# Second attention with keys on partitions: shifts in the f16 product, fp32 values and ones in column tiles, no transposes, and a reordered feed-forward

## The reference, cut to what matters

```python
q = (x @ Wq.T)                       # 8 heads of 32
kv = x @ Wkv_down.T                  # rank 64
k, v = kv @ Wk_up.T, kv @ Wv_up.T
scores = einsum('bqhd,bkhd->bhqk', q, k) * 32 ** -0.5
attn = softmax(scores, axis=-1)      # over 1024 keys
out = einsum('bhqk,bkhd->bqhd', attn, v) @ Wo.T
```

## Time and profile before

| | |
|---|---|
| median of 3 runs | 2518.78 us (2516.68 to 2521.06) |
| the profiled execution: time, span | 2519.22 us, 2517.4 us |
| granted TensorE clock, mean | 0.938 of 2.4 GHz |
| busy share of the span: PE, DVE, ACT, POOL | 87%, 84%, 72%, 49% |
| second attention, first load to the projection's first load | 1753.85 to 2320.67 us |
| first and second feed-forward, and the store of the result | 1526.2 to 1678.6 us, 2356.6 us to the end |

### The profile page before, as it was taken

The page is one execution under the profiler, slowest core; times in us unless marked ns, Lnnn a source line. Parts: engine busy times, 40 slices in busy tenths (PEclk is TensorE's granted clock), DMA queues, the critical chain, the costliest instruction groups (busy, mean ns, idle before and its releaser), DMA issues. The chain is left out here.

```text
span 2517.4 us, 62298 instructions
## 1 busy us (share of the span) xinstructions
PE 2198.9 (87%) x22572; PEld 1502.4 (60%) x22572; DVE 2116.7 (84%) x3170; ACT 1817.7 (72%) x2658; POOL 1239.9 (49%) x1482
## 2 busy tenths in 40 slices
PE   5899999999999999999999983556899999999464
PEld 3466667666667666667666663442455555555444
DVE  6899999999999999999999967755899999996674
ACT  1788888888888888888888860115899999996011
POOL 3444444444444444444444443200888888885120
PEclk9999999999999999999999996659899999999766
DMA  2799999999999999999999990006232222221001
GB/s 91 123 192 193 192 186 193 192 192 190 190 192 193 188 192 193 187 193 191 193 190 188 193 172 24 0 8 218 61 72 70 69 71 70 69 69 40 24 1 34
DMA packets 1183690, 333.53 MB, mean 132 GB/s; under 512 B 1145968, under 2 KB 1174512, under 8 KB 1183216
## 3 DMA queue, kind: packets, MB, share of 16 engines
q1 hardware_dynamic: 1182320, 326.97, 73.0%
q10 hardware_dynamic: 1152, 3.62, 0.4%
HBM read 30.57 MB, written 14.68 MB: 18 GB/s over the span
## 5 line engine op out<-in xcount | busy, mean ns | idle before, releaser
L329 PE MATMUL a_out_ps<-a_vs,a_pT 128*128 128x129 f16 x4096 | 726.0, 221 | 48.2 <-ACT a_own_out L378 46.7
L416 DVE SCALAR_TENSOR_TENSOR a_parts<-a_probs,a_parts 128x1024 f16<-128x1024 f32 x512 | 653.2, 1276 | 115.5 <-ACT a_parts L369 115.5
L333 PE MATMUL a_out_ps<-a_vs,a_pT 128*128 128x129 f16 x4096 | 724.4, 219 | 0.0
L331 PE MATMUL a_out_ps<-a_vs,a_pT 128*128 128x128 f16 x4096 | 724.3, 218 | 0.0
L361 ACT ACTIVATE a_probs<-a_score_ps,a_negmax 128x1024 f32<-128x1024 f32 x512 | 572.1, 1117 | 164.9 <-DVE a_negmax L410 164.9
L410 DVE TENSOR_REDUCE a_negmax<-a_score_ps 128x1 f32<-128x1024 f32 x512 | 621.3, 1213 | 2.5 <-PE a_score_ps L315 2.4
L369 ACT ACTIVATE a_parts<-a_probs 128x1024 f16<-128x1024 f32 x512 | 543.4, 1061 | 0.6 <-DMA a_pT<-a_parts 0.6
L329 PEld LDWEIGHTS a_out_ps<-a_vs,a_pT 128*128 128x128 f16 x4096 | 396.5, 97 | 146.1 <-ACT a_own_out L378 99.7
L331 PEld LDWEIGHTS a_out_ps<-a_vs,a_pT 128*128 128x128 f16 x4096 | 403.0, 98 | 44.6
L477 POOL TENSOR_TENSOR acc<-acc,a_own_out 128x256 f32<-128x256 f32 x256 | 248.3, 970 | 351.9 <-DVE a_parts L416 346.5
L311 PE MATMUL a_score_ps<-kh,a_qs 128*128 128x512 f16 x1024 | 388.6, 379 | 10.3 <-DVE a_qs L401 7.0
(11 more groups left out here) (200 smaller groups left out, 2737.0 us busy)
## 6 DMA issues: line engine op xcount, KB each, us to landing
a_pT<-a_parts SPq DMA_TRANSPOSE x512, 4.9
b_qs<-q_parts SPq DMA_DIRECT2D x128, 64.0 KB, 2.0
b_ks<-k_parts SPq DMA_DIRECT2D x128, 64.0 KB, 1.8
q_parts<-b_parts SPq DMA_DIRECT2D x32, 128.0 KB, 1.9
k_parts<-b_parts SPq DMA_DIRECT2D x32, 128.0 KB, 1.9
v_parts<-b_v_all SPq DMA_DIRECT2D x4, 1024.0 KB, 4.6
b_vs<-v_parts SPq DMA_DIRECT2D x32, 128.0 KB, 2.0
b_sent_pT<-b_sent_parts SPq DMA_TRANSPOSE x256, 2.3
```

The lines of the kernel that those rows point to most:

```text
L329: pe.matmul(out[:, 0:D + 1], hi, vs[:, G % 2, 0, j, 0:D + 1], start=j == 0, stop=False, skip_group_check=True)
L331: pe.matmul(out[:, 0:D], hi, vs[:, G % 2, 1, j, 0:D], start=False, stop=False, skip_group_check=True)
L333: last = pe.matmul(out[:, 0:D + 1], lo, vs[:, G % 2, 0, j, 0:D + 1], start=False, stop=j == JB - 1, skip_group_check=True)
L416: dve.scalar_tensor_tensor(out=parts[:, T % RING_P, 1, :], in0=probs[:, T % RING_P, :], scalar=PSCALE, in1=parts[:, T % RING_P, 0, :], op0 ...
```

## The change

`attend_b` is new. A unit is still 512 queries of one head, 64 in all, but its loops are written out. For each unit:

- `rate(u, t)`: for 128 queries, the scores against 1024 keys, queries on partitions, in the one tile max_ps; 96 rows of the stack (three pairs of parts). `row_max` takes the negated maximum of it (4 for each unit), and that is all that these scores are used for. After the fourth, the maxima are scaled into nm16 (f16, divided by 64).
- `spread_max`: four short products put the maxima of 512 queries on all partitions of bank 3 of score_ps; `keep_shift` copies 32 rows of it into rows 96 to 127 of qs. The same rows of ks hold 2, so that the score product subtracts the shift.
- `scores(u, pair)`: keys on partitions, 512 queries, two blocks of 128 keys for each of four pairs; `exponentiate` has no bias and no row sum, and writes fp32 probabilities that are already turned.
- `times_v(u, pair)`: for both blocks, v (fp32, kept on chip by `prepare_b` in v_all) and a block of ones are the stationary operands of four column tiles of 32 each. The ones give the denominator. `keep` takes the reciprocal of 128x128 denominators and multiplies.

GpSimd only writes two constants. Maxima run up to two units ahead. oT has the queries' four tiles on four groups of 32 partitions; `project_b` multiplies them as 32 products a chunk in four row tiles, with Wo loaded by eight DMAs.

`prepare_b` keeps v as fp32: no low parts, no store.

In the feed-forward, xh waits for the scoring products; the third `turn` moves behind the last pick, and the copy of xsel ahead of the last four of ohT; ScalarE scales half of kx, from a second product with the key weights; the normalising moves behind the product with v; the gate is one Silu activation and one product.

```diff
-def attend_b(st, q_dram, k_dram, v_dram, oT, ident):
+def attend_b(st, q_dram, k_dram, v_all, oT, ident):
...
+        max_ps = st.ps(s, "b_max_ps", [P, SEQ])
+        score_ps = st.ps(s, "b_score_ps", [P, 4, HALF])
+        out_ps = [st.ps(s, f"b_out_ps{i}", [P, 2, 2 * P]) for i in range(2)]
...
+            def rate(u, t):
...
+                if t == 0 and u % 2 == 0:
+                    pe.wait_ge(qk_in[slot], 96 * (u // 2 // SLOTS + 1))
+                if u or t:
+                    pe.wait_ge(max_ready, TILES * u + t)
+                cols = slice(u % 2 * HALF + t * P, u % 2 * HALF + (t + 1) * P)
                 for c in range(2):
+                    last = pe.matmul(max_ps[:, c * CH:(c + 1) * CH], qs[0:STACK, slot, cols],
+                                     ks[0:STACK, slot, c * CH:(c + 1) * CH], start=True, stop=True)
+                last.then_inc(rated, 1)
+
+            def spread_max(u):
...
+                pe.wait_ge(nm_ready, u + 1)
+                if u:
+                    pe.wait_ge(exp_done, PARTS * (u - 1) + 2)
+                for t in range(TILES):
+                    last = pe.matmul(score_ps[:, 3, t * P:(t + 1) * P], nm16[:, u % 2, t:t + 1].broadcast_to([P, P]),
+                                     ident16[:], start=t == 0, stop=True, skip_group_check=True)
+                last.then_inc(spread, 1)
+
+            def scores(u, pair):
+
+                if pair == 0:
+                    pe.wait_ge(shift_ready, u + 1)
+                if pair == 3 and u + 1 < units:
+                    pe.wait_ge(shift_ready, u + 2)
+                if u or pair >= 2:
+                    pe.wait_ge(exp_done, PARTS * u + pair - 1)
+                slot = u // 2 % SLOTS
+                for j in (2 * pair, 2 * pair + 1):
+                    last = pe.matmul(score_ps[:, j % 4, :], ks[:, slot, j * P:(j + 1) * P],
+                                     qs[:, slot, u % 2 * HALF:(u % 2 + 1) * HALF], start=True, stop=True)
                 last.then_inc(scored, 1)
...
+            def times_v(u, pair):
...
+                if pair == 0 and u >= 2:
+                    pe.wait_ge(kept, u - 1)
+                pe.wait_ge(exp_done, PARTS * u + pair + 1)
+                out = out_ps[u % 2]
+                for j in (2 * pair, 2 * pair + 1):
+                    for kind, left in ((0, v_all[:, u // 2, j, :]), (1, ones[:])):
+                        for t in range(TILES):
+                            last = pe.matmul(out[t * HDB:(t + 1) * HDB, 0, kind * P:(kind + 1) * P], left,
+                                             probs[:, u % 2, j, t * P:(t + 1) * P], start=j == 0 and kind == 0,
+                                             stop=j == JB - 1, skip_group_check=True)
                 last.then_inc(pv_done, 1)
...
+            for u in range(units):
+                scores(u, 0)
+                scores(u, 1)
+                rate(u + 1, 3)
+                times_v(u - 1, 2)
+                times_v(u - 1, 3)
+                spread_max(u + 1)
+                rate(u + 2, 0)
+                scores(u, 2)
+                scores(u, 3)
+                rate(u + 2, 1)
+                times_v(u, 0)
+                times_v(u, 1)
+                rate(u + 2, 2)
...
+            keep_shift(0)
+            for u in range(units):
+                exponentiate(u, 0)
+                exponentiate(u, 1)
+                keep_shift(u + 1)
+                exponentiate(u, 2)
+                exponentiate(u, 3)
...
+            for u in range(units):
+                row_max(u + 1, 3)
+                row_max(u + 2, 0)
+                keep(u - 1)
+                row_max(u + 2, 1)
+                row_max(u + 2, 2)
+            keep(units - 1)
...
             pool.wait_ge(ln.normed, NT)
+            pool.wait_ge(junked, NT)
             pool.tensor_tensor(xh[:], x[:], xn[:], ALU.add)
...
-                dve.tensor_tensor(pr_[:, pr], pr_[:, pr], rd[:, pr, :, None].broadcast_to([P, HA, CAP]),
-                                  ALU.mult).then_inc(probs_ready, 1)
             dve.wait_ge(o_done, 1)
-            dve.tensor_copy(o[:], A[:, 0:2 * D].rearrange("p (r d) -> p r d", r=2)).then_inc(o_kept, 1)
+            dve.tensor_tensor(o[:].rearrange("p r (h d) -> p r h d", h=HA),
+                              A[:, 0:2 * D].rearrange("p (r h d) -> p r h d", r=2, h=HA),
+                              rd[:, :, :, None].broadcast_to([P, 2, HA, HDA]), ALU.mult).then_inc(o_kept, 1)
...
-            act.activation(e[:], wide[0][:, 0:6 * QK].rearrange("p (c t) -> p c t", c=3), ACT.Exp,
-                           scale=-1.0).then_inc(up_exped, 1)
+            act.activation(e[:], wide[0][:, 0:6 * QK].rearrange("p (c t) -> p c t", c=3),
+                           ACT.Silu).then_inc(up_gated, 1)
...
+                for h in range(HB):
+                    u = 2 * (c // 2 * HB + h) + c % 2
+                    for t in range(TILES):
+                        rows = slice(t * HDB, (t + 1) * HDB)
+                        last = pe.matmul(y[c % 2][:, t, 0:D], oT[rows, u, :], wo[rows, h, :], start=h == 0,
+                                         stop=h == HB - 1)
```

More of the change, by code:

```diff
@@ L495, in _ @@
                     add((i - AH - 4) // 2)
-def attend_b(st, q_dram, k_dram, v_dram, oT, ident):
+def attend_b(st, q_dram, k_dram, v_all, oT, ident):
     nc = st.nc
     heads = NB * HB
[L509 to L523, removed]
-    with ExitStack() as s:
[L526 to L559, removed]
-        v_ready = st.sem("b_v_ready")
-        pool_passed, sp_passed = st.sem("b_pool_passed"), st.sem("b_sp_passed")
@@ L619, in _ @@
+            for G in range(heads):
+                slot = G % SLOTS
+                if G >= SLOTS:
+                    sp.wait_ge(scored, 2 * PARTS * (G - SLOTS + 1))
+                for part in range(3):
+                    rows = slice(part * HDB, (part + 1) * HDB)
+                    sp.dma_start(qs[rows, slot, :], q_dram[part // 2, G]).then_inc(qk_in[slot], 16)
+                    sp.dma_start(ks[rows, slot, :], k_dram[part % 2, G]).then_inc(qk_in[slot], 16)
         @block.tensor
         def _(pe):
[L621 to L635 removed]
@@ L693, in one_turn @@
-            def one_turn(n, first, last):
-                for t in range(TURN_T):
-                    if not (last and t + AHEAD_B >= TURN_T):
-                        scores(n, t + AHEAD_B)
-                    for j in (2 * t, 2 * t + 1):
-                        if j % JB not in SENT:
-                            turn(n, j)
-                        if not (first and j < LAG):
-                            times_v(n, j - LAG)
-            for t in range(AHEAD_B):
-                scores(0, t)
@@ new lines, in _ @@
+            pe.wait_ge(consts, 3)
+            for t in range(TILES):
+                rate(0, t)
+            spread_max(0)
+            for t in range(TILES - 1):
+                rate(1, t)
+            for u in range(units):
[12 more added lines that the diff above has]
+                rate(u + 2, 2)
@@ L792, in one_turn @@
-            def one_turn(n, first, last):
-                for t in range(TURN_T):
-                    if not (last and t + AHEAD_B >= TURN_T):
-                        row_max(n, t + AHEAD_B)
-                    for j in (2 * t, 2 * t + 1):
-                        if j in splits:
-                            low(n, j)
-                        elif j in dve_js:
-                            copy_block(n, j)
-                    if not (last and t + AHEAD_B > TURN_T):
-                        invert(n, t + AHEAD_B - 1)
-                    if t % 4 in (1, 2) and not (first and t < 4):
-                        keep(n if t >= 4 else n - 1, (t // 4 - 1) % UNITS, t % 4 - 1)
@@ new lines, in keep @@
+            def keep(u):
+                if u < 0:
+                    return
+                dve.wait_ge(pv_done, PARTS * (u + 1))
+                dve.reciprocal(inv[:, u % 2, :], out_ps[u % 2][:, 0, P:]).then_inc(inv_ready, 1)
+                dve.wait_ge(inv_ready, u + 1)
+                dve.tensor_tensor(oT[:, u, :], out_ps[u % 2][:, 0, 0:P], inv[:, u % 2, :], ALU.mult).then_inc(kept, 1)
+            dve.memset(ks[STACK:P, :, :], SHIFT / HDB).then_inc(consts, 1)
+            for t in range(TILES):
+                row_max(0, t)
```

398 lines of the change are left out of this document (105 added, 293 removed).

## The result

The changed kernel takes 2492.52 us (median of 3 runs, 2492.05 to 2493.61) against 2518.78: a ratio of 0.9894, 95% interval 0.9879 to 0.991. It is 26.3 us faster; 2492 was forecast. The profiled execution has a span of 2490.3 us against 2517.4.

A forecast was written before the change was run, and what follows sets the result against it. TensorE was taken to bound the second attention, other engines near behind, and chains of single steps the feed-forwards and projection. From 2519.22 us, +22.5 - 3 - 8 - 39 = -27.5 gave 2492, range 2458 to 2530.

The forecast's parts named there:

- The loop: Second attention: products and row maxima wait for each other through the single max_ps, so a unit takes 8.9 us.
- The first rival: Second attention: blocks of eight column-tile groups bind harder, 0.03 more a group erases the gain; typical 2535 us, chance 0.2.
- the second: Rival: blocks of column-tile groups don't bind, unit 8.55 us, projection 1.7 a chunk; total 2466 us, chance 0.18.
- Second attention: Whole attend_b stage: start, 62 full units of 8.9 us and end sum to 589 against 566.8, +22.5 us.
- Preparation: prepare_b: without the store of v the next stage waits only for the last k store, -3 us.
- Projection: project_b: 32 products in row tiles, 2.2 us a warm chunk, and eight loads for one; 26.6 against 34.6, -8 us.
- Feed-forward: Both feed-forwards: shorter chains of single steps save 19.5 us each, -39 us together.
- xh: Feed-forward: GpSimd's sum moved behind the scoring products lets the transposes end 8.7 us earlier and stays hidden.
- The normalising: Feed-forward: the second group of transposes need wait only for the second exponential, -4.3 us.
- the gate: Feed-forward, before the w3 products: a silu and one product replace a reciprocal and three short ones, -6.6 us.
- kx: Feed-forward: VectorE's 4.62 us halved, ScalarE scalings beside it, one more cold product ahead; -0.5 us.
- the tail: Feed-forward, end of route: two rounds of transposing and copying move behind the last pick, +0.6 us.

The follow-up runs named there:

- the ring: Changed kernel with the maxima's products going to three PSUM banks of 512 keys instead of one two-bank tile: 2413.79 us, ratio 0.958 to the kernel before.
- the direct-maxima kernel: Changed kernel with two whole maxima tiles, three single score banks, GpSimd adding pairs of exponentials, and reductions writing f16 maxima used unscaled: 2352.25 us, ratio 0.9337.

## Why the prediction was right, step by step

The mechanism that the forecast hangs on, the unit of 8.9 us and what ends each of its waits, is as predicted. That the total came within half a microsecond of 2492 is luck: the parts missed by +1.9 (attention), -2.6 (projection) and +3.1 (feed-forwards), and the first attention, which no edit touches, was 2.0 shorter; together that is 0.4. The start of the first feed-forward lies anywhere from 1542.97 to 1545.97 in the fourteen traces, so those 2.0 are scatter between executions.

**The loop, the step on which all hung.** Counting from maximum 3 (2003.46), forecast and trace: the pair before at -0.64 and -0.64; the first PV block to 1.77 and 1.78; maximum 0 at 2.63 and 2.65; maximum 1 at 5.0 and 4.98; second block from 4.5 and 4.47, the pair behind it at 6.35 and 6.36; maximum 2 at 7.0 and 7.00; the unit 8.9 and 8.92, the bare hole 0.72 and 0.70. The reciprocal takes 0.95 as interpolated, the product 0.29 for 0.28, eight groups in a row are 0.215 to 0.22 apart. The first rival needed 0.03 more a group to eat the gain and didn't come; the second needed room in the PV blocks, and they bind: without the reciprocal nothing changes, and with half their groups the unit falls to 8.52, near that rival's 8.55. That the one tile is the cause is shown by the ring.

**Second attention, +24.4 for +22.5.** The 62 full units take 553.0 for 551.8; the rest of the difference lies in the slow-clock start, about 1 us shorter than taken, and the end, about 2 us longer. One small term was off, with no effect: exponentials take 1.02 without bias and row sum, not 1.12 (no run tells which of the two costs it). ScalarE waited anyway.

**Preparation, -3.0 as forecast.** The stage begins about 1.9 after the last k store has been issued.

**Projection, -10.6 for -8.** The mis-sized term is the warm chunk: 1.79 us where I took 2.2 between 1.7 and 3.5. Four row tiles of 32 run as four column tiles do, 0.22 a group, and the weight load of each product adds nothing to that. The start was late instead: products 6.9 us after the first load for 5.9, the eight issues alone taking 5.21. The Trainium skill ("TensorE: Matmul & The Clock Gate", on packing small matmuls) gives 3.07x, for products of 512 columns, from which the estimate of 2.3 came. Here, with 128 columns, 7.0/1.79 is 3.9x, the 7.0 being itself an estimate: twice the 3.5 a chunk of before (3.57 between its additions in the trace). The measurement decides.

**Feed-forward, -18.9 and -17.0 for -19.5 each.** xh -8.6 for -8.7, shown by the run that undoes it. The normalising -4.3 as forecast, the gate -6.6 as forecast. kx came to +0.4 in the first and -1.2 in the second for -0.5, the tail to +0.7 and +2.3 for +0.6; the ranking was 1.5 longer in the second, and the W3 products 1.1 shorter in both. The terms that missed are those in which TensorE works in short bursts, where the granted clock differs from trace to trace: over the tail it was 0.88 in the first feed-forward of the kernel before, 0.84 and 0.76 in the two of the changed kernel.

**Where the gain went.** The change frees GpSimd, half of ScalarE and the transposes, and gets nothing for it in the attention, since the maxima's tile exists once and every pair of products waits for the reduction of the pair before. A third half-tile bank, paid for with one copy by a ScalarE that has time, turns the attention's +24 into -54.6 (512.2 us against 566.8 in the traces).

## What to carry to other kernels

When a change leaves every engine well under full and the stage isn't shorter, look for a buffer of which there is one: follow one period from start to start, and write beside every hole what released it. A second buffer may be had by cutting the tile, not only by finding room for a whole one. Once a wait is gone the bound moves at once to an engine (here TensorE at 7.74 us), and then taking work off that engine pays only as far as the next one in line has room for what the receiver costs it. The same sums on GpSimd brought nothing while VectorE was nearly full (7.74 to 7.80 us), and the unit fell to 6.84 once the banks were dealt so that VectorE had less to do, though it still met GpSimd in the scaling.

## What the runs showed of the hardware that I had not expected

- The same 64 write-back products take 7.45 us at a granted clock of 1.00 or 9.8 to 10.4 at 0.70 to 0.74, with no edit to them, and in one kernel one way in the first feed-forward and the other way in the second (10.11 and 7.45 in the kernel with the new feed-forward alone). Differences of 3 to 5 us between kernels with such bursts can be this alone. Executions of one kernel differ too: the five of the direct-maxima kernel go from 2349.73 us at a mean granted clock of 0.948 to 2357.8 at 0.944.
- A scaling of 128x4 with one SBUF operand (f32 in, f16 out) took 758 ns on average beside GpSimd's sums (1147 where GpSimd also had the product of keep), 169 without, while a reciprocal of 128x128 with one SBUF operand kept its 0.95 us. Which property of the two makes the difference no run here shows.
- GpSimd's sum of 128x512 takes 1.28 to 1.30 us, so 128x4096 at 8.83 is cheaper by the column: 2.16 ns against 2.5.
- A row maximum from PSUM of 128x512 takes 0.68 us and one of 128x1024 takes 1.22: halving the tile costs some 0.14 a pair.
